# A windowed-attention block on one core: the turn of the attention rows moved from round 5 to round 4

## The chip, the core and the metric

One core of a Trainium2 chip runs the whole program. The metric is the device time of one execution in microseconds (us), lower is better. The kernel before takes 2191.48 us, the median of 3 runs (2190.91 to 2192.81).

## What is computed

A Swin block on x of 32 x 56 x 56 x 64: layer norm, a shift by 3, attention with 8 heads of 8 channels in windows of 7 x 7 with a bias from relative coordinates and a mask, a projection and a residual, then a second layer norm, an MLP with hidden size 256 and an exact gelu, and a second residual.

```python
shortcut = x
y = roll(ln(x, norm1_w, norm1_b), (-3, -3))
win = windows(y)                                   # (2048, 49, 64)
q, k, v = split(win @ qkv_w.T, heads=8)
attn = softmax(q @ k.T * d ** -0.5 + bias + mask)
out = roll(unwindow((attn @ v) @ proj_w.T + proj_b), (3, 3))
x = shortcut + out
z = ln(x, norm2_w, norm2_b)
return x + gelu(z @ fc1_w.T + fc1_b) @ fc2_w.T + fc2_b
```

## The kernel before

The work is cut into 128 units of 16 windows; each engine walks over the units in program order, and each unit has 8 rounds (k = 0 to 7), one for each pair of windows. The loop is a software pipeline: in the rounds of unit i the engines also do parts of the units around it. Seen from i, the names are a = i + 1, f = i + 2, n = i + 3 (units being prepared) and c = i - 1, d = i - 2, e = i - 3, g = i - 4 (units being finished). All order between engines is by semaphores, written out by hand.

In each round TensorE (PE) does, in this order: `scores` (L722, q times k into the one bank S, with two mask matmuls of L726 in some rounds), `scores_T` (L738, the same transposed into ST, for the round two back), a step that belongs to this round, `shift` (L744, adds the negated row maxima nmd into ST), and `times_v` (L758, for the round four back, into O). `scores` of a round wait until VectorE (DVE) has reduced those of the round before (`neg_max`, L582, writes nm). GpSimd (POOL) spreads nm to nmd (L326), and ScalarE (ACT) takes the exponential of ST (L426). Rounds 3 and 7 of every unit have mask matmuls of half width, and in the units with i % 4 == 3 those of rounds 4 to 7 have full width ("full masks").

The step of its own is, by round: 0 turn of z, turn back and q/k projection; 1 v projection; 2 and 3 the two halves of fc1 of unit e; 4 turn of y of unit f, and at the round's end, behind `times_v`, fc2 of unit e; 5 the turn of the attention rows of unit c; 6 the output projection of unit c. A turn is four TensorE transposes by `turn_tokens` (L766) into a bank of M: y into bank 1, z into bank 2, the attention rows `on` into bank 3.

The four banks of M are shared. `fc1_high` writes banks 2 and 3, and ACT's second `gelu` (L445, c = 1) reads them. ACT counts s_g once for each gelu, two for each unit; both gelus of unit e come in its round 2, behind that round's exponential and a load of the activation table, and another table load comes before the next exponential. `turn_y` waits for the first gelu (s_g at 2e + 1), since bank 1 is read by it. DVE's `normalise(c, 1)` (L588, L592) makes the second half of `on` in round 4, ahead of `neg_max` of that round. ACT's `evac_oT` (L433, its round 4, behind the exponential) takes bank 3 to oT, and `project_out` (L814) reads that in round 6. `fc2` waits for both gelus. SyncE moves q and k between partitions with DMAs (hl to qp and kp), and ACT's `high_parts` (L407) waits until the ones of the unit before have landed.

Of the kernel before, what the change touches and what calls it, by code (L numbers as in the profile page):

```python
# [43 lines left out]
def swin_block(nc, x, c_vec, c_weights, c_projb, c_keys, c_diag, c_shift, out):  # L44
    NSB = x.shape[0]
    ctx = ExitStack()
    with ctx:
# [6 lines left out]
        def sem(name):  # L54
            return ctx.enter_context(nc.semaphore(name))
# [127 lines left out]
        s_g = sem("s_g")  # L183
# [12 lines left out]
        def on_chip(u):  # L196
            return not isinstance(u, int) or 0 <= u < NSB
# [14 lines left out]
        def at_unit(i, k, back):  # L212
            return i + (k - back) // U, (k - back) % U
# [465 lines left out]
        def _(pe):  # L679
# [5 lines left out]
            def keep_running(n):  # L685
                zeros = mT[:].rearrange("c w n -> c (w n)")
                for _ in range(n):
                    MM(M[W0:W0 + N, 3, 0:HT], zeros[:, 0:N], zeros[:, 0:HT],
                       start=True, stop=True, tile_position=(0, W0))
# [18 lines left out]
            def scores(u, r, j):  # L708
                b = j // 4
                if later(u) or j >= 1:  # L710
                    pe.wait_ge(s_nm, U * u + j)
                if j % 4 == 0:
                    pe.wait_ge(s_q[r % 2][b], 128 * (u // 2) + 128)
                    if not later(u, 2):
                        pe.wait_ge(c_q[u % 2][b], 1)
                        pe.wait_ge(c_keys_in[u % 2][b], 16)
                q, key, v = qp[r % 2][b], kp[r % 2][b], variant(r, j)
                for w in range(2):
                    t = slice(span(j) + N * w, span(j) + N * w + N)
                    for hp in range(4):  # L720
                        for e in range(2):
                            mm = MM(S[W0 * e:W0 * e + N, N * (4 * w + hp):N * (4 * w + hp + 1)], q[:, 2 * hp + e, t],  # L722
                                    key[:, 2 * hp + e, t], start=(w == 0 and hp == 0), stop=(v == 0), skip_group_check=True)
                first = 0 if v >= 2 else 4
                for e in range(2 if v else 0):
                    mm = MM(S[W0 * e:W0 * e + N, N * first:HK], shiftw[:, v, 2, :],  # L726
                            diag[:, first:8, :].rearrange("r h n -> r (h n)"), start=False, stop=True, skip_group_check=True)
                mm.then_inc(s_sc, 1)

            def scores_T(u, r, j):  # L730
                q, key = qp[r % 2][j // 4], kp[r % 2][j // 4]
                if later(u) or j >= 2:
                    pe.wait_ge(s_e, U * u + j - 1)
                for w in range(2):
                    t = slice(span(j) + N * w, span(j) + N * w + N)
                    for hp in range(4):
                        for e in range(2):
                            MM(ST[W0 * e:W0 * e + N, j % 2, N * (4 * w + hp):N * (4 * w + hp + 1)], key[:, 2 * hp + e, t],  # L738
                               q[:, 2 * hp + e, t], start=(w == 0 and hp == 0), stop=False, skip_group_check=True)
# [23 lines left out]
            def turn_tokens(bank, src, sem_out):  # L763
                tokens = src[:].rearrange("r p c -> r (p c)")
                for q in range(4):
                    mm = nc.tensor.transpose(M[:, bank, 2 * W0 * q:2 * W0 * q + R], tokens[:, 2 * C * q:2 * C * q + 2 * C],  # L766
                                             ident[0:R, 0:R])
                mm.then_inc(sem_out, 1)
# [9 lines left out]
            def project_qk(u, d):  # L778
                pe.wait_ge(s_yT, u + 1)
                if on_chip(d):  # L780
                    pe.wait_ge(s_att, d + 1)
                for h in range(2):
                    rows = slice(C * h, C * h + C)
                    mm = MM(M[:, h, 0:HT], wqk[rows, :], yT[rows, :], start=True, stop=True)  # L784
                mm.then_inc(s_qk, 1)

            def room_for_v(u, e, g):
                if on_chip(e):
                    pe.wait_ge(s_zT, e + 1)
                elif later(u):  # L790
                    pe.wait_ge(s_vx, 2 * u)
                if on_chip(g):
                    pe.wait_ge(s_res, g + 1)

            def project_v(u):
                for s in range(8):
                    for e in range(2):
                        mm = MM(M[W0 * e:W0 * e + N, 2, C * s:C * s + C], yT[:, N * s:N * s + N], wv[:, e, :],  # L798
                                start=True, stop=True, tile_position=(0, W0 * e))
                mm.then_inc(s_vp, 1)  # L800

            def turn_o(u, e, a):
                pe.wait_ge(s_on, 2 * u + 2)
                if not on_chip(e):
                    pe.wait_ge(s_vx, 2 * a + 2)
                turn_tokens(3, on, s_oTp)

# [10 lines left out]
            def turn_z(u, e, a):  # L818
                pe.wait_ge(s_z1, u + 1)
                if on_chip(e):  # L820
                    pe.wait_ge(s_mT, e + 1)
                elif on_chip(a):
                    pe.wait_ge(s_vx, 2 * a + 2)
                turn_tokens(2, z1, s_zTp)
# [7 lines left out]
            def fc1_low(u, a, d):  # L832
                pe.wait_ge(s_zT, u + 1)
                if on_chip(a):
                    pe.wait_ge(s_lo, a + 1)
                elif on_chip(d):
                    pe.wait_ge(s_att, d + 1)
                fc1(u, 0)
# [16 lines left out]
            def turn_back(u):  # L855
                pe.wait_ge(s_mT, u + 1)
                src = mT[:].rearrange("c w n -> c (w n)")
                for q in range(4):
                    mm = nc.tensor.transpose(M[0:R, 3, 2 * C * q:2 * C * q + 2 * C], src[:, 2 * W0 * q:2 * W0 * q + R],  # L859
                                             ident[:])  # L860
                mm.then_inc(s_mo, 1)

            def body(i, m):
                a, f, c, d, e, g = i + 1, i + 2, i - 1, i - 2, i - 3, i - 4
                if i == -2:
                    pe.wait_ge(c_weights_in, 16)
                    pe.wait_ge(c_scaled, 1)
                if i == 0:
                    pe.wait_ge(c_const_in, 48)
                for k in range(U):  # L870
                    u2, j2 = at_unit(i, k, 2)
                    r2 = m if k >= 2 else m + 3
                    u4, j4 = at_unit(i, k, 4)
                    r4 = m if k >= 4 else m + 3
                    if k == 0 and on_chip(e):
                        turn_z(e, g, i)
                    if k == 0 and on_chip(g):
                        turn_back(g)
                    if i == -2 and k in (0, 5) or i == 0 and k in (2, 3, 5, 6, 7):
                        keep_running(1)  # L880
                    if i == -1 and k == 5:
                        keep_running(5)
                    if on_chip(i):
                        scores(i, m, k)
                    if k == 1 and on_chip(a):
                        room_for_v(a, e, g)
                    if on_chip(u2):
                        scores_T(u2, r2, j2)
                    if k == 0 and on_chip(a):
                        project_qk(a, d)  # L890
                    if k == 1 and on_chip(a):
                        project_v(a)
                    if k == 2 and on_chip(e):
                        fc1_low(e, a, d)
                    if k == 3 and on_chip(e):
                        fc1_high(e, a, g)
                    if k == 4 and on_chip(f):
                        turn_y(f, e)
                    if k == 5 and on_chip(c):
                        turn_o(c, e, a)  # L900
                    if k == 6 and on_chip(c):
                        project_out(c, f)
                    if on_chip(u2):
                        shift(u2, r2, j2)
                    if on_chip(u4):
                        times_v(u4, r4, j4)
                    if k == 4 and on_chip(e):
                        fc2(e)

            for i in range(-3, NSB + 4):  # L910
                body(i, i % 4)
# [89 lines left out]
```

## Time and profile before

| | |
|---|---|
| median of 3 runs | 2191.48 us |
| profiled execution | 2191.34 us |
| its span | 2189.5 us |
| TensorE busy | 2140.3 us (98%) |
| TensorE weight loads busy | 1667.7 us (76%) |
| VectorE busy | 1780.1 us (81%) |
| ScalarE busy | 1545.3 us (71%) |
| GpSimd busy | 1772.9 us (81%) |

Busy time is the union of an engine's instructions. Weight loads run beside matmuls and are a row of their own (PEld). Matmuls are pipelined, and the end shown for one is modelled, so that neighbouring groups overlap in the records; the start-to-start time of two groups is what a group costs. In a timeline, a row is a group of like instructions: start, time from the first start to the last end, engine, line, operation, written and read tiles, shapes and count. A bracket behind it gives the engine's idle time ahead of it and what ended it.

### The profile page before, as it was taken

Reading aid. Unit: us, or ns where it says so; the run is one execution under the profiler, and the core shown is the slowest. Engines: PE = TensorE matmul, PEld = TensorE weight load, DVE = VectorE, ACT = ScalarE, POOL = GpSimd, SP = SyncE. Lnnn points to the kernel's source line nnn. Section 1 sums busy time; section 2 is a strip of 40 time slices with the busy share of each in tenths; the row PEclk is TensorE's granted clock in tenths of the full one; section 3 lists DMA queues with packets and bytes.
Section 4 is the critical chain, followed back from the end, with each engine's and each line's share of the span. In section 5 each row is a group of like instructions: output and inputs, shape, how many; then the busy total and the mean of one; then the engine's idle time right before and its main releaser. Section 6 shows DMA issues by size and latency. Waiting matters only on the chain.

```text
span 2189.5 us, 148006 instructions
## 1 busy us (share of the span) xinstructions
PE 2140.3 (98%) x62790; PEld 1667.7 (76%) x62790; DVE 1780.1 (81%) x3231; ACT 1545.3 (71%) x2435; POOL 1772.9 (81%) x1687
## 2 busy tenths in 40 slices
PE   6999999999999999999999999999999999999997
PEld 3777777777777777777777777777777777777775
DVE  5788888888888888888888888888888888888874
ACT  4577777677677777767777776776777777777774
POOL 5788888888888888888888888888888888888874
PEclk8999999999999999999999999999999999999999
DMA  4232233222323332232323223233223333322321
GB/s 111 65 78 78 75 75 76 77 77 76 79 74 76 76 76 77 75 79 76 77 76 76 77 75 77 78 75 79 75 77 77 76 77 76 77 76 76 77 70 32
DMA packets 178587, 165.86 MB, mean 76 GB/s; under 512 B 21144, under 2 KB 152458, under 8 KB 178074
## 3 DMA queue, kind: packets, MB, share of 16 engines
q1 hardware_dynamic: 178074, 157.60, 28.0%
q8 instruction: 495, 8.11, 1.6%
q14 instruction: 18, 0.15, 0.0%
HBM read 28.99 MB, written 25.77 MB: 25 GB/s over the span
## 4 chain that ended last, share of the span: by engine, by line
PE 88%; DVE 4%; issue 3%; ACT 2%; SPq 2%; DMA 1%; DVEq 0%; POOL 0%; ACTq 0%; POOLq 0%
PE O L758 14%; PE S L722 11%; PE ST L744 10%; PE M L766 9%; PE ST L738 9%; PE M L829 9%; PE M L851 8%; PE M L814 5%; PE M L798 5%; PE M L784 4%; PE M L859 2%; PE S L726 2%; SPq L274 1%; DVE nm L582 1%; ACT gl L445 1%
## 5 line engine op out<-in xcount | busy, mean ns | idle before, releaser
L326 POOL TENSOR_TENSOR nmd<-diag,nm 121x392 f16<-121x392 f16 x1024 | 900.3, 892 | 288.1 <-DVE nm L582 234.1
L582 DVE TENSOR_REDUCE nm<-S 121x8 f16<-121x392 f32 x1024 | 574.3, 561 | 225.7 <-PE S L722 138.3
L426 ACT ACTIVATE pT<-ST 113x392 f32<-113x392 f32 x1024 | 506.9, 496 | 229.7 <-PE ST L744 224.9
L758 PEld LDWEIGHTS O<-vx,pT 113*49 113x49 f32 x16384 | 548.6, 126 | 45.1 <-issue 6.1
L758 PE MATMUL O<-vx,pT 113*49 113x18 f32 x16384 | 522.2, 196 | 3.8 <-issue 1.9
L722 PE MATMUL S<-kp,qp 128*49 128x49 f16 x16384 | 390.7, 186 | 11.0 <-DVE nm L582 7.9
L738 PE MATMUL ST<-qp,kp 128*49 128x49 f16 x16384 | 387.0, 185 | 2.4 <-issue 2.3
L722 PEld LDWEIGHTS S<-kp,qp 128*49 128x49 f16 x16384 | 313.0, 103 | 93.1 <-issue 55.5
L744 PE MATMUL ST<-nmd,shiftw 121*49 121x392 f16 x2048 | 354.4, 342 | 0.2 <-POOL nmd L326 0.2
L738 PEld LDWEIGHTS ST<-qp,kp 128*49 128x49 f16 x16384 | 324.8, 103 | 10.2 <-issue 2.3
L407 ACT ACTIVATE hl<-M 128x784 f16<-128x784 f32 x128 | 105.5, 824 | 309.1 <-PE M L784 229.3
L744 PEld LDWEIGHTS ST<-nmd,shiftw 121*49 121x49 f16 x2048 | 108.7, 102 | 246.8 <-issue 122.5
L346 POOL TENSOR_TENSOR xres<-xin,projb 113x512 f32<-113x512 f32 x128 | 205.2, 1603 | 78.6 <-DVE res L634 78.5
L829 PE MATMUL M<-zT,weights 64*128 64x392 f32 x1024 | 237.9, 540 | 2.0 <-DVE zT L627 1.5
L445 ACT ACTIVATE gl<-M,vec 128x784 f32<-128x784 f32 x256 | 220.0, 911 | 4.0 <-PE M L829 2.5
L353 POOL TENSOR_TENSOR rstd<-veps,mhalf 113x8 f32<-113x8 f32 x128 | 210.8, 1647 | 13.9 <-DVE veps L621 13.9
L333 POOL TENSOR_TENSOR rstd<-veps,mhalf 113x8 f32<-113x8 f32 x128 | 209.7, 1638 | 10.5 <-DVE veps L562 10.5
L851 PE MATMUL M<-gl,weights 128*64 128x392 f32 x1024 | 195.1, 503 | 4.9 <-ACT gl L445 4.9
L417 ACT ACTIVATE vx<-M 49x512 f32<-49x512 f32 x256 | 154.8, 605 | 17.1 <-PE M L798 4.6
L426 ACT ACT_TABLE_LOAD x126 | 161.7, 1283 | 2.2
L445 ACT ACT_TABLE_LOAD x126 | 161.7, 1283 | 2.2
L600 DVE TENSOR_TENSOR xres<-M,xres 113x512 f32<-113x512 f32 x128 | 88.6, 692 | 72.7 <-PE M L814 72.7
(90 smaller groups left out, 3369.2 us busy)
## 6 DMA issues: line engine op xcount, KB each, us to landing
qp<-hl SPq DMA_DIRECT2D x1024, 49.0 KB
kp<-hl SPq DMA_DIRECT2D x1024, 49.0 KB
xin<-in_x SPq DMA_DIRECT2D x256, 98.0 KB
out<-res SPq DMA_DIRECT2D x256, 98.0 KB
kp<-in_c_keys SPq DMA_DIRECT2D x4, 588.0 KB, 7.2
weights<-in_c_weights SPq DMA_DIRECT2D x1, 448.0 KB, 4.4
bias_t<-spread SPq DMA_DIRECT2D x2, 73.5 KB, 2.2
shiftw<-in_c_shift SPq DMA_DIRECT2D x1, 139.0 KB
```

The source lines that it names most:

```text
L326: nc.gpsimd.tensor_tensor(nmd[j % LAG][:], diag[:], nm[j % LAG][:].unsqueeze(2).broadcast_to([RM, 2 * 4, N]), ALU.mult).then_inc(s_nmd, 1)
L333: nc.gpsimd.tensor_tensor(rstd1[:], veps1[:], mhalf[:], ALU.pow).then_inc(s_rs1, 1)
L353: nc.gpsimd.tensor_tensor(rstd2[:], veps2[:], mhalf[:], ALU.pow).then_inc(s_rs2, 1)
L426: nc.scalar.activation(pT[j % LAG][:].rearrange("k w h q -> k (w h q)"), ST[0:R, j % 2, 0:HK], ACT.Exp).then_inc(s_e, 1)
L445: nc.scalar.activation(gl[:, c], M[:, 2 * c:2 * c + 2, 0:HT], ACT.Gelu, bias=b1[:, c:c + 1]).then_inc(s_g, 1)
L582: V.tensor_reduce(nm[j % LAG][:], S[0:RM, 0:HK].rearrange("q (h n) -> q h n", n=N), AX_X, ALU.max, negate=True).then_inc(s_nm, 1)
L722: mm = MM(S[W0 * e:W0 * e + N, N * (4 * w + hp):N * (4 * w + hp + 1)], q[:, 2 * hp + e, t], key[:, 2 * hp + e, t], start=(w == 0 and hp == ...
L738: MM(ST[W0 * e:W0 * e + N, j % 2, N * (4 * w + hp):N * (4 * w + hp + 1)], key[:, 2 * hp + e, t], q[:, 2 * hp + e, t], start=(w == 0 and hp ...
L744: mm = MM(ST[W0 * e:W0 * e + N, j % 2, 0:HK], shiftw[:, variant(r, j), e, :], nmd[j % LAG][:].rearrange("r h n -> r (h n)"), start=False, ...
L758: mm = MM(O[W0 * w:W0 * w + N, (4 * p + hp) * VC:(4 * p + hp + 1) * VC], pT[j % LAG][:, w, hp, :], vx[r % RING][:, window + 2 * w, hp, :], ...
L829: mm = MM(M[:, 2 * c + h, 0:HT], w1[rows, 128 * c:128 * c + 128], zT[rows, :], start=True, stop=True)
L851: mm = MM(M[C * h:C * h + C, 2, 0:HT], w2[:, c, :], gl[:, c, h, :], start=(c == 0), stop=(c == 1), tile_position=(0, C * h), skip_group_ch ...
```

## The change

The call of `turn_o` moves from round 5 to round 4, directly behind `turn_y` and ahead of `shift`, `times_v` and `fc2` of that round. Where unit e exists, `turn_o` now also waits for both gelus of e (s_g at 2e + 2), since it writes bank 3 of M in a round that fc2, which had that wait, only ends. Its wait for both halves of `on` stays, and so does the wait that stands where there is no unit e.

```diff
             def turn_o(u, e, a):
                 pe.wait_ge(s_on, 2 * u + 2)
-                if not on_chip(e):
+                if on_chip(e):
+                    pe.wait_ge(s_g, 2 * e + 2)
+                else:
                     pe.wait_ge(s_vx, 2 * a + 2)
                 turn_tokens(3, on, s_oTp)
...
                     if k == 4 and on_chip(f):
                         turn_y(f, e)
-                    if k == 5 and on_chip(c):
+                    if k == 4 and on_chip(c):
                         turn_o(c, e, a)
                     if k == 6 and on_chip(c):
                         project_out(c, f)
```

## Rows read from the trace of the kernel before

**Rows 1.** Busy time by stretch: stretch, its length, busy us (instructions) of PE, PEld, DVE, ACT, POOL, clock, DMA.
```profile
1357.50:1423.60 66.10, 65.91 (x1965) 51.61 (x1959) 55.39 (x101) 47.91 (x77) 55.13 (x52) 1.00 0.30 77
94.51:2119.10 2024.59, 2012.40 (x59723) 1576.23 (x59721) 1684.59 (x3048) 1466.40 (x2319) 1680.58 (x1586) 1.00 0.30 76
```

**Rows 2.** Timeline of TensorE, rounds 4 to 6 of a usual unit.
```profile
1057.81 0.37 PE L738 MATMUL ST<-qp,kp 128*49 128x49 f16 x16
...
1058.22 0.58 PE L766 MATMUL M<-weights,y 113*128 113x113 f32 x4
...
1058.73 0.35 PE L744 MATMUL ST<-nmd,shiftw 121*49 121x392 f16 x2
...
1059.27 1.51 PE L851 MATMUL M<-gl,weights 128*64 128x392 f32 x8
...
1060.61 0.37 PE L722 MATMUL S<-kp,qp 128*49 128x49 f16 x16
1060.82 0.38 PE L738 MATMUL ST<-qp,kp 128*49 128x49 f16 x16
...
1061.13 0.61 PE L766 MATMUL M<-weights,on 113*128 113x113 f32 x4
...
1061.67 0.35 PE L744 MATMUL ST<-nmd,shiftw 121*49 121x392 f16 x2
...
1062.20 0.37 PE L722 MATMUL S<-kp,qp 128*49 128x49 f16 x16
```

**Rows 3.** Timeline of ScalarE in the same unit: both gelus together, and the second alone.
```profile
1057.16 1.72 ACT L445 ACTIVATE gl<-M,vec 128x784 f32<-128x784 f32 x2
...
1057.97 0.91 ACT L445 ACTIVATE gl<-M,vec 128x784 f32<-128x784 f32 x1
```

**Rows 4.** Timeline of VectorE and TensorE in the same unit, rounds 2 to 5.
```profile
1054.88 0.35 PE L744 MATMUL ST<-nmd,shiftw 121*49 121x392 f16 x2
...
1054.98 0.55 DVE L582 TENSOR_REDUCE nm<-S 121x8 f16<-121x392 f32 x1
...
1055.59 0.40 PE L722 MATMUL S<-kp,qp 128*49 128x49 f16 x16
...
1058.20 0.42 DVE L592 TENSOR_TENSOR on<-O,rec 113x256 f32<-113x256 f32 x1
...
1061.03 0.57 DVE L582 TENSOR_REDUCE nm<-S 121x8 f16<-121x392 f32 x1 [1.34 <-PE S L722]
```

**Rows 5.** Timeline of a unit with full masks, rounds 4 to 6.
```profile
1023.84 1.72 ACT L445 ACTIVATE gl<-M,vec 128x784 f32<-128x784 f32 x2
...
1024.99 0.61 PE L766 MATMUL M<-weights,y 113*128 113x113 f32 x4
...
1027.41 0.37 PE L722 MATMUL S<-kp,qp 128*49 128x49 f16 x16
...
1028.00 0.57 DVE L582 TENSOR_REDUCE nm<-S 121x8 f16<-121x392 f32 x1 [1.60 <-PE S L726]
...
1029.17 0.37 PE L722 MATMUL S<-kp,qp 128*49 128x49 f16 x16
```

**Rows 6.** Timeline of TensorE, round 7 and the start of round 0.
```profile
1047.94 0.37 PE L738 MATMUL ST<-qp,kp 128*49 128x49 f16 x16
1048.15 0.33 PE L744 MATMUL ST<-nmd,shiftw 121*49 121x392 f16 x2
...
1048.75 0.60 PE L766 MATMUL M<-weights,z 113*128 113x113 f32 x4
1049.19 0.60 PE L859 MATMUL M<-weights,mT 128*113 128x128 f32 x4
```

**Rows 7.** Waits: engine and line, what it waited for, us in total, times, the longest.
```profile
ACT hl L407 <- PE M L784: 229.3, 98, 2.7
...
ACT hl L407 <- DMA kp<-hl: 79.8, 29, 5.0
```

**Rows 8.** Busy time of VectorE alone, neg_max of round 7 to that of round 2.
```profile
1048.15:1055.53 7.38, 7.31 (x14) 1.00 0.32 76
```

## The prediction

> **What bounds the kernel now.** I first read the busy time by stretch [rows 1]. Four units from turn of y to turn of y, with nothing unusual in them, take 66.10 us, 16.53 us each, and TensorE (PE) is busy for 65.91 us of that, at a granted clock of 1.00, the 2.4 GHz level. So PE sets the pace, and a change of order on PE can only bring something by removing a gap or by adding one. But "busy" hides small gaps, because the modelled end of a matmul lies 0.16 us or so behind the start of the next group. So the second view is PE's own order of time [rows 2], read from start to start. There the group that turns y begins 0.41 us after the scores_T group ahead of it (1057.81 to 1058.22), where the same kind of group ahead of the turn of the attention rows takes 0.31 (1060.82 to 1061.13). That is a real wait of 0.10 us, on ScalarE (ACT): the first gelu starts at 1057.16 and one gelu takes 0.91 [rows 3], so it ends at 1058.07, and the turn starts 0.15 us later. In a unit with the full masks (every fourth) PE arrives last: its turn of y starts at 1024.99, and both gelus have ended by 23.84 + 1.72 = 1025.56 [rows 5], 0.57 us after it. In the usual unit they have ended by 57.16 + 1.72 = 1058.88, 0.66 us after the start of the turn. These two distances, 0.66 and 0.57, are what the change meets.
>
> Third, VectorE (DVE). PE's scores of a round wait for neg_max of the round before (one S bank). In round 3 this binds: nm starts at 1054.98 and takes 0.55, and the scores start at 1055.59, 0.06 us after its end, 0.71 us after the start of the shift ahead of them (1054.88) [rows 4], where shift and times_v give way after 0.53 in round 5 (1061.67 to 1062.20) [rows 2]: a wait of 0.18. So DVE to PE costs 0.06 us, ACT to PE 0.15.
>
> **What the change moves.** Four transposes of "on" leave round 5 and stand in round 4 behind the four of y; one wait is added, for both gelus (bank 3 of M is read by the second one). Nothing else of any queue is moved. Behind the waiting instruction on PE stand shift, times_v and fc2 of round 4 and then the scores of round 5, for which DVE waits.
>
> Step 1, the usual unit, counted from the start of the turn of y (T). Before: the turn gives way after 0.51, shift and times_v take 0.54, fc2 1.34, and the scores of round 5 start at T + 2.39 (1060.61) [rows 2]. After: the turn of y would be through at T + 0.44, as the turn of z is when another transposing group follows it (1048.75 to 1049.19) [rows 6]. The two waits of the new turn end at: normalise, 1058.20 + 0.42 = T + 0.40, plus 0.06 = T + 0.46 [rows 4]; second gelu, T + 0.66 + 0.15 = T + 0.81. The gelu is last. PE stands for 0.37 us, then turns "on" (0.51, as a turn that had to wait does), then 0.54 and 1.34: the scores of round 5 start at T + 3.20, 0.81 later than before.
>
> Step 2, what comes back in round 5. Before, the scores of round 6 start 1.59 us after those of round 5 [rows 2]. Without the turn PE needs only 0.21 (scores), 0.21 (scores_T directly ahead of a shift, 1047.94 to 1048.15 [rows 6], where it took 0.31 ahead of the turn) and 0.53 (shift and times_v, 1061.67 to 1062.20): 0.95. So the turn gives back 0.64, and not just its own 0.54.
>
> Step 3, the new wait. The scores of round 6 need neg_max of round 5. It starts 0.42 after the scores (1060.61 to 1061.03), takes 0.57 [rows 4], and PE follows 0.06 later: 1.05 us, more than 0.95. DVE, which had over a microsecond of idle time ahead of this nm, becomes the last by 0.10 us. Round 6 then starts at T + 4.25, against T + 3.98 (2.39 + 1.59): 0.27 us later in each usual unit.
>
> Step 4, the unit with full masks. Before: scores 5 at 1027.41, T + 2.42, scores 6 at 1029.17, T + 4.18 [rows 5]. After: 0.57 + 0.15 + 0.51 + 0.54 + 1.34 = T + 3.11; nm starts 0.59 behind the scores (1028.00), plus 0.57 and 0.06: T + 4.33. 0.15 us later.
>
> Step 5, does the delay stay? The waits of the rest of the unit hang on PE itself: DVE works without a pause from neg_max of round 7 to that of round 2 (7.31 us of 7.38 [rows 8]), which begins when PE's scores of round 7 are there, and the gelus hang on PE's shift of round 2. So a PE that comes 0.27 us later moves everything by 0.27. The covers that could break hold: exp of round 4 waits for a shift that now starts at T + 1.32 and not at T + 0.51, but until then ACT has the second gelu, the reload of its table and the exp of round 3 ahead of it; fc2's result and the shifts' nmd are not due for rounds. The attention rows reach ACT two microseconds earlier, but project_out does not wait now (it starts where PE's order lets it), so this is worth nothing. DVE's neg_max of round 6 comes behind ln1_var and has some 0.2 us left before round 7 needs it.
>
> Step 6, the sum. 125 units have both the gelus and scores of their own: 93 x 0.27 + 32 x 0.15 = 29.9 us. In the last two of them there is no turn of y to take part of the wait for the gelus, some 0.6 us more each: 1.2. The first two units have no gelu and change nothing.
>
> Step 7, what a longer unit loosens. The 122 units between the turns of y at 94.51 and 2119.10 take 2024.59 us; by the four quiet ones they would take 122 x 16.525 = 2016.05 [rows 1]. The 8.5 us between are units in which ACT's high_parts waits for the landing of kp: 29 times, 2.75 us in the mean, where it stands 2.34 us for PE in the others, so these are late by some 0.41 [rows 7]. A unit longer by 0.24 us leaves the transfers that much more room, which covers 0.24 of 0.41, a share of 0.59. Between nothing and 8.5 us may come back; I take 0.59 x 8.5 = 5.
>
> Against the profiled execution (2191.34 us, its span 2189.5 and 1.8 around it; the median 2191.48 is the same within 0.01%): 2191.3 + 29.9 + 1.2 - 5 = 2217.4.
>
> A rule that speaks against the change stands in the Trainium skill, page "TensorE: Matmul & The Clock Gate", Part 4, PE-mode transpose: transposes do not count as activity for PE's clock, so two turns and a wait in a row would be a hole for the clock gate. By it the clock could fall in rounds 4 and 5. The trace has the same pair already, turn of z and turn back, from 1048.75 to the end of 1049.19 + 0.60, more than a microsecond [rows 6], at a granted clock of 1.00 [rows 1], so it does not bear this out; the sum by it would be rival F's.
>
> **The rivals.**
> A, the forecast: the gelu wait and the neg_max wait both cost. 2217.4; with nothing or all of the 8.5 us back, and 0.05 us a unit either way, 2208 to 2229.
> B, the gelu wait costs, the neg_max wait does not (scores of round 6 by PE's own 0.95): usual unit 3.20 + 0.95 - 3.98 = 0.17, masked 3.11 + (1.76 - 0.64) - 4.18 = 0.05. 93 x 0.17 + 32 x 0.05 + 1.2 = 18.6, less up to 8.5: 2201 to 2210. Against it: round 3 shows that wait to the hundredth.
> C, both are worse: the signals take 0.15 us instead of 0.06 behind DVE, and neg_max of round 6, pushed behind ln1_var, delays round 7 by another 0.1 us: 125 x 0.19 = 24 more, 2241.
> D, it is taken up again: the waits ahead of the turn of y (0.10) and of the scores of round 3 (0.18) shrink by as much as the unit grew. 0.27 - 0.28 = 0: 2191, within 0.2%. Against it stand rows 8 and the fixed chain from shift to gelu.
> E, faster: the second gelu ends by T + 0.29 and not at T + 0.66, so that turning "on" waits for nothing. This is the point from which it decides. Then y gives way after 0.44, "on" after 0.54, the scores of round 5 start at T + 2.86, those of round 6 at T + 3.91: 0.07 us earlier, masked units 0.10: 93 x 0.07 + 32 x 0.10 = 9.7, 2182. What speaks for it is that two turns in a row are cheaper than two apart; against it, the gelus hang on PE and their pair takes 1.72 us [rows 3], so the second can't end so soon.
> F, the clock falls in round 4 and 5 of each unit: a granted clock of half for the 3.2 us would add at most as much again, hundreds of microseconds. Nothing in these rows shows it.
>
> **How the numbers follow.** A 0.62, B 0.15, C 0.10, D 0.07, E 0.05, F 0.01. A measurement of this kernel can tell about 0.2% (4.4 us) from no change. Slower by more than that: A, B, C and F, 0.88; within: D, 0.07; faster: E, 0.05. The range takes A's bounds, most of B and the near half of C: 2203 to 2236.
>
> **What would show it.** In the changed profile: a turn of "on" that starts 0.81 us after the turn of y in usual units and 0.72 in masked ones, with ACT's gl as what ended the wait (step 1); 0.95 to 1.05 us from scores 5 to scores 6, and DVE's nm named ahead of them (steps 2, 3); four quiet units of 66.10 + 3 x 0.27 + 0.15 = 67.1 us (step 6); fewer waits of high_parts for kp (step 7). Wrong it would be if the turn of "on" followed at 0.44, or if the gap ahead of the turn of y closed.

## The result and the profile after

The changed kernel takes 2221.68 us, the median of 4 runs (2221.52 to 2225.1), beside 2191.9 for the kernel before: 29.8 us more, a ratio of 1.0137 with a 95% interval of 1.0121 to 1.0152. Slower, as forecast: 1.4%, small but clear of the noise. The median lies 4.3 us above the predicted 2217.4, inside the range. Its profiled execution is the longest of the four (2225.1, span 2223.3), 33.8 us above the profiled one of before, so what follows is split up against that.

The first view, busy time by stretch (columns as in [rows 1]): four quiet units (units in which every group takes its usual time), and the 122 units from the turn of y that is made in unit 3 to the one made in unit 125.

```profile
1378.53:1445.62 67.09, 66.13 (x1965) 51.57 (x1959) 55.29 (x101) 48.16 (x77) 55.30 (x52) 1.00 0.30 75
95.66:2154.15 2058.49, 2018.94 (x59727) 1575.15 (x59721) 1679.07 (x3048) 1468.18 (x2319) 1685.77 (x1586) 1.00 0.30 75
```

Against [rows 1], four quiet units take 67.09 us where they took 66.10, and now TensorE's idle time shows: 66.13 busy of 67.09. The granted clock is 1.00 as before. 0.99 / 4 x 122 = 30.2 us is the pattern itself. The stretch as a whole has grown by 33.9, so what lies beyond its quiet units has grown too, from 8.5 to 2058.49 - 122 x 16.7725 = 12.2 us. That is in the longest of the four executions; the other three are some 3.5 us shorter.

TensorE, ScalarE and VectorE in rounds 4 to 6 of a usual unit, which answers to [rows 2 to 4]:

```profile
1073.71 0.58 PE L766 MATMUL M<-weights,y 113*128 113x113 f32 x4
...
1074.51 0.58 PE L766 MATMUL M<-weights,on 113*128 113x113 f32 x4 [0.23 <-ACT gl L445]
...
1075.02 0.35 PE L744 MATMUL ST<-nmd,shiftw 121*49 121x392 f16 x2
...
1076.90 0.37 PE L722 MATMUL S<-kp,qp 128*49 128x49 f16 x16
...
1077.32 0.57 DVE L582 TENSOR_REDUCE nm<-S 121x8 f16<-121x392 f32 x1 [2.15 <-PE S L722]
...
1077.94 0.39 PE L722 MATMUL S<-kp,qp 128*49 128x49 f16 x16
```

The turn of the attention rows starts 0.80 us after the turn of y. The bracket says 0.23 us of idle time, ended by ACT's gelu; by starts TensorE stood 0.80 - 0.44 = 0.36, because 0.13 of it lies under the modelled end of the turn of y. The scores of round 5 follow at T + 3.19 and those of round 6 only 1.04 later, 0.05 after neg_max has ended (1077.32 + 0.57 = 1077.89). No bracket names this wait, since the modelled end of times_v lies over it: it shows only from start to start. The masked unit, which answers to [rows 5]:

```profile
1107.54 0.60 PE L766 MATMUL M<-weights,y 113*128 113x113 f32 x4
...
1108.26 0.58 PE L766 MATMUL M<-weights,on 113*128 113x113 f32 x4
...
1110.65 0.37 PE L722 MATMUL S<-kp,qp 128*49 128x49 f16 x16
...
1111.24 0.57 DVE L582 TENSOR_REDUCE nm<-S 121x8 f16<-121x392 f32 x1 [2.29 <-PE S L726]
...
1111.86 0.39 PE L722 MATMUL S<-kp,qp 128*49 128x49 f16 x16
```

There it is 0.72 us between the turns, T + 3.11 and T + 4.32. The list of waits (waiting engine and line, what it waited for, us in total, times, the longest) has a group that came to 3.0 us in 14 waits before and is now in almost every unit, and it has fewer waits for kp, 18 where [rows 7] has 29:

```profile
ACT hl L407 <- DMA kp<-hl: 53.8, 18, 6.5
...
PE M L766 <- ACT gl L445: 29.7, 118, 1.9
```

### The profile page after: what moved, and what is told of

It is laid out like the page before. It is cut to its first block, busy times and chain, and to the rows that moved or that the text cites. A ratio compares the mean times of both kernels' runs of the same rounds, so it can differ in the third digit from the quotient of the medians.

```text
span 2223.3 us, 148132 instructions
## 1 busy us (share of the span) xinstructions
PE 2145.5 (97%) x62790; PEld 1665.8 (75%) x62790; DVE 1774.2 (80%) x3231; ACT 1547.2 (70%) x2435; POOL 1778.3 (80%) x1687
## 4 chain that ended last, share of the span: by engine, by line
PE 79%; ACT 7%; issue 6%; DVE 4%; SPq 1%; ACTq 1%; DMA 1%; DVEq 0%; POOL 0%; POOLq 0%
PE O L758 12%; PE S L722 10%; PE ST L744 9%; PE M L853 8%; PE ST L738 8%; PE M L831 8%; PE M L766 7%; PE M L816 5%; ACT gl L445 5%; PE M L798 5%; PE M L784 4%; PE M L861 2%; ACT L445 2%; PE S L726 2%; SPq L274 1%
## 5 line engine op out<-in xcount | busy, mean ns | idle before, releaser
L359 POOL TENSOR_TENSOR z<-z,rstd 113x512 f32<-113x512 f32 x128 | 133.6, 1044 | 10.0
```

## The experiments

The table sets beside each measured time what the pattern of four quiet units gives, (length - 66.10) / 4 x 122. The runs were made on several chips, each beside the kernel before on the same chip, so the differences and ratios can be compared and the bare times of different rows can't. Four quiet units differ by up to 0.3 us within a trace. In e1 the value shown is at the low end: the usual time of each of the four kinds of unit, over the 122 units, adds up to 66.19 there, which is +2.7. Where a kernel has a line more ahead of the part shown, its line numbers are one or two higher.

| kernel | four quiet units, us | by the pattern | measured against before | ratio (95%) |
|---|---|---|---|---|
| changed | 67.09 | +30.2 | +29.8 | 1.0137 (1.0121 to 1.0152) |
| changed, again (e9) | 67.08 | +29.9 | +34.9 | 1.0161 (1.0147 to 1.0176) |
| changed, short gelu (e1) | 66.04 | -1.8 | -1.0 | 0.9994 (0.9985 to 1.0004) |
| before, short gelu (e2) | 66.10 | 0.0 | -0.7 | 0.9995 (0.9985 to 1.0005) |
| changed, short maximum (e3) | 66.53 | +13.1 | +19.1 | 1.0083 (1.0066 to 1.0100) |
| changed, both short (e5) | 65.27 | -25.3 | -22.8 | 0.9879 (0.9857 to 0.9901) |
| turn behind times_v (e4) | 66.52 | +12.8 | +16.6 | 1.0080 (1.0059 to 1.0100) |
| changed, half the bytes (e6) | 67.07 | +29.6 | +28.2 | 1.0121 (1.0099 to 1.0143) |
| before, half the bytes (e7) | 66.09 | -0.3 | -4.1 | 0.9973 (0.9963 to 0.9983) |
| shift first (e8) | 65.91 | -5.8 | -3.3 | 0.9981 (0.9969 to 0.9993) |
| ln2_var later (e10) | 65.98 | -3.7 | -1.6 | 0.9994 (0.9985 to 1.0003) |
| both (e11) | 65.73 | -11.3 | -10.0 | 0.9963 (0.9949 to 0.9976) |

**The wait for the second gelu.** In the changed kernel the second gelu is made short:

```diff
-                nc.scalar.activation(gl[:, c], M[:, 2 * c:2 * c + 2, 0:HT], ACT.Gelu,
+                wide = HT if c == 0 or not later(u) else HT // 4
+                nc.scalar.activation(gl[:, c, :, 0:wide], M[:, 2 * c:2 * c + 2, 0:wide], ACT.Gelu,
```

> The changed kernel, in which the second gelu of each unit but the first reads and writes only a quarter of its columns (the MLP's result is then not the reference's). Theory (the cost is the wait of the turn of the attention rows for the second gelu): that gelu now ends before T + 0.29, the turn waits only for normalise (T + 0.40 and 0.06) and starts at T + 0.46 and not at T + 0.81; scores of round 5 at T + 2.86, scores of round 6 (still held by neg_max, 1.04 later) at T + 3.90, 0.08 us ahead of the kernel before. 93 x 0.08 + 32 x 0.10 = 11 us under the kernel before: 2181, and 40 under the changed one. Rival (two turns in a row or the wait as such cost, whatever ends it): it stays above 2210. Rival (the gelu's wait is taken over by another wait): the turn starts later than T + 0.5, and its releaser is named.

Measured: 2187.38 us beside 2188.41. Its timeline:

```profile
1040.46 0.58 PE L767 MATMUL M<-weights,y 113*128 113x113 f32 x4
...
1040.91 0.61 PE L767 MATMUL M<-weights,on 113*128 113x113 f32 x4
...
1043.33 0.37 PE L723 MATMUL S<-kp,qp 128*49 128x49 f16 x16
...
1044.37 0.39 PE L723 MATMUL S<-kp,qp 128*49 128x49 f16 x16
...
1044.93 0.84 POOL L326 TENSOR_TENSOR nmd<-diag,nm 121x392 f16<-121x392 f16 x1
1044.94 0.86 DVE L563 TENSOR_SCALAR veps<-ss 113x8 f32<-113x8 f32 x1
...
1045.71 0.55 DVE L583 TENSOR_REDUCE nm<-S 121x8 f16<-121x392 f32 x1
...
1046.32 0.40 PE L723 MATMUL S<-kp,qp 128*49 128x49 f16 x16
```

The turn follows at T + 0.45, scores 5 at T + 2.87, scores 6 at T + 3.91, all as expected, so the gelu's end is what made the turn stand. But the gain did not last: scores 7 come 1.95 after scores 6, where they came 1.83 later. VectorE's neg_max of round 6 stands behind ln1_var (ss and veps) and ends at 1046.26, and the scores of round 7 start 0.06 after it. And ln1_var is late because veps, a small instruction, takes 0.86 us here, where it takes 0.54 in a usual unit of the changed kernel (from 1078.51). It ends 0.03 us after GpSimd's nmd, which started beside it. This is no accident of one unit: of 120 such instructions in each of the 13 traces, 1533 of 1560 end 0.02 to 0.035 us after a GpSimd instruction, and the usual time of veps goes from 0.26 us (e5) to 0.86 (e1) with the place of that instruction. So the two turns in a row are cheaper on TensorE, as the arithmetic had it, and VectorE takes that back. That GpSimd's instruction holds veps is read from these ends; no edit tested it.

The control, the same edit in the kernel before:

> Control for the run above: the kernel before with the same short second gelu. In it only fc2 waits for the second gelu, at T + 1.05, and it has ended by T + 0.66. Theory: 2192, no change within 3 us. Rival (a shorter gelu helps in itself, through ScalarE's later work): clearly under 2185, and then the run above says less.

Measured: 2187.7 us, ratio 0.9995 (0.9985 to 1.0005). The shorter gelu is worth nothing by itself, so the distance between the changed kernel and e1, some 31 us by the ratios 1.0137 and 0.9994 (37 from the ratio of e9), is the wait and what hangs on it.

**The wait for neg_max.** In the changed kernel neg_max of round 5 reads every second key:

```diff
-                V.tensor_reduce(nm[j % LAG][:], S[0:RM, 0:HK].rearrange("q (h n) -> q h n", n=N),
+                step = 2 if j == 5 else 1
+                V.tensor_reduce(nm[j % LAG][:], S[0:RM, 0:HK].rearrange("q (h n) -> q h n", n=N)[:, :, 0:N:step],
```

> The changed kernel, in which neg_max of round 5 reads every second key only (25 of 49 a head), so that it is about 0.2 us shorter (the maximum is then not the exact one). Theory (0.09 us a unit of the loss is the scores of round 6 waiting for neg_max of round 5): scores 5 to scores 6 falls from 1.04 to TensorE's own 0.95, 125 x 0.09 = 11 us: 2210. Rival (the wait shown there is not binding, TensorE is as slow without it): 2221, and the distance stays at 1.04.

Measured: 2207.51 us, ratio 1.0083 against 1.0137: 12 us less than the changed kernel (17 by the quiet units, and 17 against the ratio of e9), where 11 were expected. Scores 5 to scores 6:

```profile
1050.84 0.37 PE L723 MATMUL S<-kp,qp 128*49 128x49 f16 x16
...
1051.78 0.37 PE L723 MATMUL S<-kp,qp 128*49 128x49 f16 x16
```

0.94 where it was 1.04. So the wait that no bracket named is real, and has the size that was read from start to start. The same edit was not run in the kernel before. There, in the unit of [rows 4], neg_max of round 5 ends at 1061.60, 0.60 us ahead of the scores of round 6, so nothing on TensorE waits for it in that place.

With both short:

> The changed kernel with both shortenings: the second gelu on a quarter of its columns, and neg_max of round 5 on every second key (neither result is exact then). The short gelu alone brought it level with the kernel before and not 11 us under it: scores 6 came 0.07 us earlier, but scores 7 then waited 0.10 for neg_max of round 6, which stands behind ln1_var. Theory (from round 5 on VectorE's chain is what ends last): neg_max of round 5 0.2 us shorter moves ln1_var and neg_max of round 6 forward too, both waits go, scores 5 to 6 takes 0.95 and 6 to 7 takes 1.83; scores 7 come 0.17 us a unit earlier than in the kernel before: ratio to before 0.990. Rival (the 0.10 at round 7 is something else, such as the transposed rows or the output projection): ratio 0.995 or more, with times_v of round 6 still giving way after 0.45.

Measured: 2165.44 us, 0.9879. A usual unit:

```profile
1051.54 0.37 PE L724 MATMUL S<-kp,qp 128*49 128x49 f16 x16
...
1052.48 0.37 PE L724 MATMUL S<-kp,qp 128*49 128x49 f16 x16
...
1054.31 0.38 PE L724 MATMUL S<-kp,qp 128*49 128x49 f16 x16
```

0.94 and 1.83: both waits are gone. With two results cut short, the new order is thus worth some 23 us, and 53 us lie between that and what it costs. How much of the 23 the shorter maximum would bring without the change was not run; the slack of 0.60 us suggests little of it.

**The place.** The turn stays in round 4 but behind times_v, where the gelu has ended:

```diff
-                    if k == 4 and on_chip(c):
-                        turn_o(c, e, a)
...
                     if on_chip(u4):
                         times_v(u4, r4, j4)
+                    if k == 4 and on_chip(c):
+                        turn_o(c, e, a)
```

> The changed kernel with the turn of the attention rows in round 4, but behind shift and times_v and ahead of fc2; the same waits, the same work. Theory (the place costs only through what stands between it and the second gelu): shift and times_v cover the gelu (T + 0.81) until T + 1.05, or T + 1.14 with the longer change from times_v to a turn; the turn takes 0.44 ahead of fc2, scores 5 start at T + 2.93 and, with neg_max behind them, scores 6 at T + 3.97, as before (3.98), masked units 0.02 earlier: 2190 to 2192. So all of the loss goes though round 4 still holds the turn. Rival (a turn in round 4 costs because it pushes fc2 and the scores of round 5): 2210 or more.

Measured: 2204.97 us, ratio 1.0080. Neither value: the loss falls from 29.8 us to 16.6, so not all of it goes.

```profile
1046.76 0.58 PE L766 MATMUL M<-weights,y 113*128 113x113 f32 x4
1047.27 0.35 PE L744 MATMUL ST<-nmd,shiftw 121*49 121x392 f16 x2
1047.45 0.50 PE L758 MATMUL O<-vx,pT 113*49 113x18 f32 x16
1047.89 0.61 PE L766 MATMUL M<-weights,on 113*128 113x113 f32 x4
1048.42 1.54 PE L853 MATMUL M<-gl,weights 128*64 128x392 f32 x8
1049.79 0.38 PE L722 MATMUL S<-kp,qp 128*49 128x49 f16 x16
```

No wait is left, but the turn gives way to fc2 after 0.53 and not 0.44 (that was read ahead of the turn back, with weights 113 columns wide; fc2's are 64), and fc2 takes 1.37 for 1.34. Scores 5 start at T + 3.03 and not 2.93, and neg_max puts scores 6 1.04 behind them: T + 4.07, 0.09 later than before. What is left of the loss is the order of the groups and the neg_max wait, 13 us by the pattern.

**What lies beyond the quiet units.** The DMAs from hl to qp and kp move half their bytes, in the changed kernel and in the kernel before:

```diff
+                wide = T // 2 if later(u, 2) else T
...
-                        part = hl[C * qk:C * qk + C, s, b].rearrange("m a t -> m (a t)")
-                        sp.dma_start(dst[BIAS + D * n:BIAS + D * n + D], part).then_inc(s_q[r % 2][b], 16)
+                        part = hl[C * qk:C * qk + C, s, b].rearrange("m a t -> m (a t)")[:, 0:wide]
+                        sp.dma_start(dst[BIAS + D * n:BIAS + D * n + D, :, 0:wide], part).then_inc(s_q[r % 2][b], 16)
```

> The changed kernel with the DMAs that spread q and k (hl to qp and kp) moving half their bytes from the third unit on, in the same number of DMAs (the attention is then wrong in half of the columns). It tests the term of the forecast that failed: the 8 to 14 us of a run that lie beyond its quiet units. If these come from kp landing late for high_parts, they shrink by most of that: 8 to 11 us under the changed kernel, ratio to before about 1.009, and no wait of high_parts for a DMA is left. If TensorE pauses on its own in them (pauses within a group, with no semaphore in the program there), the waits for the DMA go and the time stays within 3 us of the changed kernel, ratio 1.013.

> The same halving in the kernel before. Late landings as the cause: 6 to 8 us under the kernel before. TensorE's own pauses: within 3 us of it.

Measured: 2216.41 us, ratio 1.0121 (1.0099 to 1.0143), and 2184.13 us, ratio 0.9973 (0.9963 to 0.9983). First the changed kernel, then the kernel before, by stretch (the first of each is four quiet units), and the wait for kp in it:

```profile
344.71:411.78 67.07, 66.08 (x1959) 51.53 (x1959) 54.97 (x101) 48.15 (x77) 55.28 (x52) 1.00 0.20 51
92.42:2143.43 2051.01, 2016.94 (x59722) 1573.59 (x59721) 1681.59 (x3048) 1468.78 (x2319) 1684.89 (x1586) 1.00 0.19 51
...
ACT hl L408 <- DMA kp<-hl: 7.7, 2, 4.9
```

```profile
589.73:655.82 66.09, 65.89 (x1958) 51.55 (x1959) 55.10 (x101) 48.17 (x77) 55.13 (x52) 1.00 0.20 52
92.36:2111.51 2019.15, 2010.96 (x59723) 1574.39 (x59721) 1686.06 (x3048) 1468.77 (x2319) 1680.96 (x1586) 1.00 0.20 52
...
ACT hl L408 <- DMA kp<-hl: 18.0, 6, 5.1
```

The pattern is untouched. Beyond the quiet units lie 2051.01 - 122 x 16.7675 = 5.4 us (12.2 with whole DMAs) and 2019.15 - 122 x 16.5225 = 3.4 us (8.5). These are single executions, and the remainder varies between them: e2, with the pattern of the kernel before, has 5.3. The medians over many executions are the firmer sign: 4.1 us less in e7, clear of the noise, and in the changed kernel 3.5 us less by the ratio 1.0137 (not clear of it) or 8.8 by that of e9. So a good part of the remainder hangs on the DMA traffic, and neither expectation holds in full.

But kp landing late is not the way. The quiet units of [rows 1] themselves hold two of the 29 waits for it, and each of the four has its usual time. From ScalarE's waits in that stretch of the kernel before:

```profile
ACT hl L407 <- DMA kp<-hl: 5.2, 2, 2.6
```

Of the 27 such waits in the 122 units of the kernel before, 23 stand in units less than 0.1 us longer than others of their kind. All 27 units together hold 1.9 of the 8 us. With the change there are fewer such waits (18 against 29) and more time beyond the quiet units.

What does hold time is pauses of TensorE inside a group of matmuls, where the program has no semaphore, here in the changed kernel:

```profile
1946.07 0.85 PE L798 MATMUL M<-weights,yT 128*49 128x64 f32 x22
1947.41 0.48 PE L798 MATMUL M<-weights,yT 128*49 128x64 f32 x9 [0.49 <-issue]
```

They come back at the same place of the program. In e9, the same kernel in another execution, this one stands in the same unit, behind the same 22 recorded matmuls and with the same length:

```profile
1945.34 0.48 PE L798 MATMUL M<-weights,yT 128*49 128x64 f32 x9 [0.49 <-issue]
```

Of the 13 pauses over 0.1 us in the changed kernel's profile 6 recur in e9 in the same group of the same unit, and all 5 of e2 are in this sense among the 11 of the kernel before.

And they go together with the loading of instructions. The traces have a DMA queue of its own for it (q8, packets of 16 KB, one every 4.2 us or so). In the same 122 units of all 13 traces there are 132 such pauses, and every one ends 1.2 to 1.7 us after a packet of this queue has ended (1.58 in the first one above). Only 12% of the time lies that far behind a packet, and of the waits for the gelu in the changed kernel 4% end there. With half the bytes on the other queue there are 5 pauses instead of 13 and 15 (1.4 us instead of 4.2 and 4.4), and 4 instead of 11 and 5 in the kernel before (1.2 us instead of 3.3 and 1.9). That the load makes TensorE pause is read from this coincidence and was not tested by an edit of its own. Pauses inside a group are also only a part of the remainder.

**The changed kernel again**, as the base for kernels on the chip of the last two:

> The changed kernel once more, on the chip of the runs below, as the base of the comparisons with its variants. Theory (four quiet units of 67.07 us where the kernel before has 66.10, over 122 units, and the end): ratio to before 1.0137, as before; with the quiet part of an execution the same within 1 us, and only the part beyond the quiet units different.

Measured: 2225.47 us, ratio 1.0161 (1.0147 to 1.0176). It lies above the first interval, though the two intervals overlap. By stretch:

```profile
583.80:650.88 67.08, 66.08 (x1959) 51.53 (x1959) 55.30 (x101) 47.96 (x77) 55.32 (x52) 1.00 0.29 76
94.61:2152.91 2058.30, 2018.06 (x59722) 1574.81 (x59721) 1679.00 (x3048) 1468.75 (x2319) 1686.18 (x1586) 1.00 0.30 75
```

The pattern repeats to 0.01 us, and 12.4 us lie beyond it, as in the first profile (12.2).

**Do waits hang together, or does each cost for itself?** In the kernel before, ln2_var is moved behind neg_max of round 2, which takes away the wait of the scores of round 3:

```diff
                             low_parts(a)
-                        if on_chip(d):
-                            ln2_var(d)
+                    if k == 2 and on_chip(d):
+                        ln2_var(d)
```

> The kernel before with ln2_var on VectorE moved from behind neg_max of round 1 to behind neg_max of round 2, so that neg_max of round 2 comes 1.4 us sooner and the wait of the scores of round 3 (0.16) goes. Theory of the waits (the gelus hang on TensorE's shift of round 2 and end at a fixed distance behind it, so the turn of y can't start sooner): the 0.16 is taken up again ahead of the turn of y, whose wait grows from 0.11 to 0.27; only masked units, where TensorE came last there, gain, some 0.1 each: 2 to 5 us, ratio 0.998 to 0.999. Rival (each wait costs on its own, and 0.16 saved is 0.16 a unit): 20 us, ratio 0.991.

Measured: 2188.97 us, ratio 0.9994 (0.9985 to 1.0003): no change that can be told from none, and the 20 us of the rival are out. Round 4 in it:

```profile
1040.50 0.37 PE L738 MATMUL ST<-qp,kp 128*49 128x49 f16 x16
1041.10 0.58 PE L766 MATMUL M<-weights,y 113*128 113x113 f32 x4 [0.23 <-ACT gl L445]
```

From scores_T to the turn of y it takes 0.60, where it took 0.41 [rows 2]: what was saved in round 3 is lost again in front of the gelu.

**Filling the wait that was there before.** In the kernel before, shift goes ahead of the turn of y in round 4:

```diff
+                    if k == 4 and on_chip(u2):
+                        shift(u2, r2, j2)
                     if k == 4 and on_chip(f):
                         turn_y(f, e)
...
-                    if on_chip(u2):
+                    if k != 4 and on_chip(u2):
                         shift(u2, r2, j2)
```

> The kernel before with one change: in round 4 the shift stands ahead of the turn of y, so that it fills the time in which the turn waits for the first gelu. By starts: scores_T 0.21, shift 0.17 and 0.09 for the change to a turn, so the turn of y starts at T + 0.05 (T: its start in the kernel before) and then 0.51, 0.35 and 1.35 bring the scores of round 5 to T + 2.26, against 2.39; masked units, where TensorE came last, 0.03. Theory: 93 x 0.13 + 32 x 0.03 = 13 us less, ratio 0.994. Rival (a turn takes its 0.09 on both sides, or the turn's new place between an f16 and an f32 group costs as much as the wait did): no change, ratio 0.999 to 1.001. Rival (rounds 5 to 6 are held by VectorE as in the changed kernel): no, since the turn of the attention rows still fills them with 1.59 us.

Measured: 2184.88 us, ratio 0.9981 (0.9969 to 0.9993): 3 us, not 13. The order of the groups costs again what was not in the sum:

```profile
1054.27 0.60 PE L766 MATMUL M<-weights,y 113*128 113x113 f32 x4
1054.80 0.55 PE L758 MATMUL O<-vx,pT 113*49 113x18 f32 x16
1055.19 1.52 PE L851 MATMUL M<-gl,weights 128*64 128x392 f32 x8
```

The turn takes 0.53 ahead of times_v where 0.51 was reckoned, and times_v 0.39 for 0.35. With ln2_var moved as well:

> Both together: shift ahead of the turn of y in round 4, and ln2_var behind neg_max of round 2. Theory: with the shift in front the turn of y was TensorE-bound by about 0.05 us, so 0.05 of the 0.16 saved now counts in a usual unit before the gelu is the last again, and 0.16 in a masked one; with the 0.08 a unit that the shift in front gave: 93 x 0.13 + 32 x 0.2 = 18 us less, ratio 0.992, the fastest of the exact kernels here. Rival (as above, full gains): 0.99 or less. Rival (neither adds to the other): 0.998.

Measured: 2180.59 us, ratio 0.9963 (0.9949 to 0.9976). Not much over half of what was expected, but the two edits do add up, and this kernel, which computes all that the reference asks for, beats the kernel before by 10 us and the changed one by 45.

## Why the prediction was right, and where not

- **What bounds the kernel** held. TensorE now stands at two places (0.36 and 0.10 us in a usual unit), the new order of its groups saves 0.19, and that is the growth of some 0.27. The granted clock stays at 1.00, though two turns in round 4 now have a wait of 0.36 us between them. So the rule about transposes and the clock gate, which the prediction weighed from the Trainium skill ("TensorE: Matmul & The Clock Gate", Part 4, PE-mode transpose), does not show here. Rival F falls.
- **Step 1** held: the turn at T + 0.80 (0.81 forecast), scores 5 at T + 3.19 (3.20). e1 shows by intervention that the gelu's end is the cause.
- **Steps 2 and 3** held: 1.04 (1.05), and e3 takes out the 0.10. Only the sign to look for was wrong: the forecast wanted neg_max named as the releaser, and the modelled ends hide it.
- **Step 4** held: 0.72, T + 3.11, T + 4.32 (4.33).
- **Step 5** held: the delay stays, since later waits hang on TensorE itself. e10 shows the same tie in the other direction. Rival D falls. Neg_max of round 6 has the 0.2 us left that was forecast: it ends at 1079.52, and the scores of round 7 start at 1079.79.
- **Step 6** held in its main term: 67.09 for four units (67.1), 30.2 us over 122 units. Its small term, 1.2 us for the last two units, was wrong. There the turn of the attention rows does wait longer for the gelu (it starts at 2171.55, 1.16 us after scores_T, where 0.31 is the least). But in the kernel before times_v already stood at that place, since it waited for `on` (0.42 us), and the forecast left that out:

```profile
2136.03 0.55 PE L758 MATMUL O<-vx,pT 113*49 113x18 f32 x16 [0.42 <-DVE on L592]
```

  From scores_T of round 4 to the scores of round 6 that unit takes 4.58 us (2170.39 to 2174.97) where it took 4.29 (2135.07 to 2139.36): 0.29 more, like any other, and not 0.87.
- **Step 7 failed.** It gave back 5 us of the 8.5 beyond the quiet units, on the ground that these are units in which kp lands late for high_parts and that longer units leave the transfers room. The waits for kp did become fewer, 18 for 29, and nothing came back. The premise was wrong: 2.75 us against 2.34 is how long ScalarE waited, and not what the unit lost. Most units with such a wait are not longer at all, and two of them stand in the quiet stretch of [rows 1]. What the remainder does contain is pauses of TensorE, each 1.2 to 1.7 us behind an instruction load. Both profiles of the changed kernel have more beyond the quiet units (12.2 and 12.4 us) than those with the order of before (8.5, and 5.3 in e2). The times leave open whether it grew: the growth of the pattern alone, 29.9 by steps 3 and 4, meets the first comparison (29.8), and lies 5.0 under e9 (34.9), whose interval begins at some 32.
- **The two wrong terms partly cancel.** 1.2 and -5 together took 3.8 us from a sum that without them would have been within 0.1 us of the first comparison, so the distance of the prediction is theirs. That they have opposite signs is luck.
- **Rival B** (no neg_max wait) is refuted by e3. Of **rival C**, the second half, neg_max of round 6 behind ln1_var, did not come in the changed kernel, where scores 7 come on time, but it is what ate the gain in e1. **Rival E** would have been wrong even on its own condition: with the gelu out of the way e1 gave -1.0 us and not -9.7, since the sum stopped at round 6, and neither VectorE's next items nor the GpSimd instruction beside veps was followed.

What stays open is whether and how other DMA traffic delays TensorE through the instruction loads, why the pauses sit where they do, what the rest of the remainder is, and whether the change really adds to it.

## What to carry to other kernels

On an engine that is busy to 98%, moving a step costs or gives what the waits at its new place cost, and these are read from start to start: brackets of idle time leave out what lies under a modelled end (0.13 of 0.36 us here, and all of the neg_max wait). A step that is placed in front of work that used to cover its operand's producer takes that cover away, and the queue behind it pays, here twice: once for the gelu, once since a shorter round no longer covers the reduction that the next one needs. And when a wait is taken away, follow the chain for two rounds, not one, before counting the gain. Last, the length of a wait on an engine off the critical path is not what the kernel loses by it: before pricing such waits, look whether the units that have them are longer.

## What was not expected of the hardware

A group of matmuls on TensorE has no fixed length; it depends on the group that follows it. Four transposes give way after 0.44 us to another turn or to the turn back, after 0.53 or 0.54 to shift, times_v or fc2, and after 0.51 to shift when the turn itself had to wait. times_v gives way after 0.35 to scores or fc2, 0.44 to a turn, and 0.39 to fc2 when it stands behind a turn; scores_T after 0.21 to shift, 0.31 to a turn. These hundredths, not in the first sums, are most of what e4 and e8 fell short by (0.10 us a unit in e4, 0.06 of 0.08 in e8).

TensorE pauses inside groups of matmuls of a long program without loops: 132 pauses of over 0.1 us in the 13 traces, all ending 1.2 to 1.7 us behind a packet of the instruction queue, several of them in the same group of the same unit in two executions of a kernel, and in the changed kernel fewer when other DMAs move half their bytes (5 for 13 and 15).

A VectorE instruction on 8 columns (veps) took from 0.26 to 0.86 us, and ended 0.02 to 0.035 us after the GpSimd instruction beside it in 1533 of 1560 cases.
